# Graph attention over 412,500 edges: chunks of 1024 edges in place of 512

## Chip, cores, metric

One core of a Trainium2 chip runs the whole kernel. The time is the device time in microseconds from the start to the end of one execution. A version's time is the median of several runs.

## The reference

A graph has 12,500 nodes with 96 features, and 412,500 edges sorted by their destination. Each edge has 96 features of its own. There are 8 heads of 12 features.

```
Q, K, V = x @ Wq + bq, x @ Wk + bk, x @ Wv + bv        # per node
E       = edge_attr @ We + be                          # per edge
score   = exp(clip(sum_head(K[src] * Q[dst] / sqrt(12) * E), -5, 5))
wV      = segment_sum(V[src] * score, dst);  Z = segment_sum(score, dst)
out     = layernorm(x + wV / (Z + 1e-6))
```

## The kernel before

**Stages.** First the node tables are made: TensorE turns x and projects it; keys and values go to a table in DRAM (`kv_table`), queries as three bf16 parts to another (`q_table`). Beside it the destinations are loaded, turned and made relative to each chunk's least destination. Then comes the main loop over 806 chunks of 512 edges (`CHUNK`, 128 partitions by `G` = 4 edges), and last the output stage over 25 batches of 500 nodes: division, residual and layer norm.

**One chunk in the main loop.** The edges of a chunk have destinations in a window of `WIN` = 32 nodes, since they are sorted.
- SyncE loads edge features (`ea`) and destinations (`dst_b`) for half a ring, 4 chunks, at a time, and per chunk the query rows of the window (`q_win`, 106 rows). It may load when TensorE's step count says that the slots are free (L394).
- GpSimd gathers keys and values of the sources: one indirect DMA of 128 rows for each of the 4 edges of a partition (L530). It may do so when the message product of the chunk 8 before is done (L521). The indices are loaded by ScalarE's queue, 4 chunks at a time.
- ScalarE copies the turned edge features out of PSUM (`eaT`, L760), makes the matrix that selects each edge's query from the window (`away`, L765, then `ohT`, L768), and takes the exp of the scores (L757).
- TensorE turns the edge features (L631), projects them with We (L633), multiplies the selection by the window's queries (L640), and sums messages by destination with a 0/1 matrix (L647).
- VectorE multiplies keys by queries (L907) and by the projection (L915), adds within heads (L926), clips (L938), makes the 0/1 matrix `oh` (L910) and the messages (L919), and adds a chunk's sums to the accumulator (L934).

**Order.** Each engine's program is written out by hand in `step(s, u, ...)`, and `run_steps` puts 8 (ScalarE and GpSimd: 16) steps in a loop's body. In its step s TensorE turns chunk s, projects and selects for chunk s - 2 (`PROJ_LAG`), and sums chunk s - 5 (`SUM_LAG`); turning and projecting alternate matmul by matmul. The buffers between the engines are double. One signal is sent at the end of the step, and VectorE, ScalarE and SyncE all wait for that one:

```
                last.then_inc(pe_step, 1)                       # L650, TensorE
                dve.wait_ge(pe_step, a + PROJ_LAG + 1)          # L903, VectorE
                act.wait_ge(pe_step, s + 1)                     # L753, ScalarE
                at_least(pe, kqe_done, c - 1)                   # L628, TensorE waits for VectorE
```

VectorE makes the message of chunk s - 1 in the step in which it scores chunk s. ScalarE's step is exp of chunk s - 3, copy, measure and select of chunk s. A f32 matmul is two instructions with a weight load each (L633, L647), a transpose (L631) or a bf16 matmul (L640) one with one.

## Time and profile before

| | us |
|---|---|
| median of 3 runs | 5353.9 (5344.9 to 5357.64) |
| profiled execution | 5341.94 |
| its span, first to last instruction | 5340.3 |
| TensorE busy | 3563.3 (67%) |
| GpSimd busy | 3143.5 (59%) |
| VectorE busy | 2090.0 (39%) |
| ScalarE busy | 1722.8 (32%) |

The busy times are shares of one execution's span and overlap each other. A line name as L530 is a line of the kernel. PE is TensorE, PEld its weight loads, DVE VectorE, ACT ScalarE, POOL GpSimd, SP SyncE; a q behind the name means that the engine's sequencer acts, as when it issues a DMA.

### The profile page before, as it was taken

Reading aid. Unit: us, or ns where it says so; the run is one execution under the profiler, and the core shown is the slowest. Engines: PE = TensorE matmul, PEld = TensorE weight load, DVE = VectorE, ACT = ScalarE, POOL = GpSimd, SP = SyncE. Lnnn points to the kernel's source line nnn. Section 1 sums busy time; section 2 is a strip of 40 time slices with the busy share of each in tenths; the row PEclk is TensorE's granted clock in tenths of the full one; section 3 lists DMA queues with packets and bytes.
Section 4 is the critical chain, followed back from the end, with each engine's and each line's share of the span. In section 5 each row is a group of like instructions: output and inputs, shape, how many; then the busy total and the mean of one; then the engine's idle time right before and its main releaser. Section 6 shows DMA issues by size and latency. Waiting matters only on the chain.

```text
span 5340.3 us, 72730 instructions
## 1 busy us (share of the span) xinstructions
PE 3563.3 (67%) x19972; PEld 3422.0 (64%) x19973; DVE 2090.0 (39%) x5996; ACT 1722.8 (32%) x3602; POOL 3143.5 (59%) x3249
## 2 busy tenths in 40 slices
PE   7666666666666666666666666666666666666664
PEld 6666666666666666666666666666666666666663
DVE  4333334333333333333333433333334333433346
ACT  4332333323332332333233332333333232323337
POOL 4556656665666656656665666566566665666560
PEclk7555555555555555555555555555555555555555
DMA  7444444444444444444444444444444444444442
GB/s 227 107 109 110 119 109 109 111 118 109 109 111 117 110 108 111 116 111 109 111 116 112 109 112 113 113 109 111 110 118 109 110 115 113 109 110 116 112 109 84
DMA packets 497768, 607.49 MB, mean 114 GB/s; under 512 B 256053, under 2 KB 420224, under 8 KB 497630
## 3 DMA queue, kind: packets, MB, share of 16 engines
q0 software_dynamic: 155200, 318.39, 22.5%
q1 hardware_dynamic: 233215, 281.36, 18.0%
q10 hardware_dynamic: 109330, 7.48, 1.5%
q8 instruction: 9, 0.15, 0.0%
q14 instruction: 14, 0.11, 0.0%
HBM read 584.51 MB, written 22.46 MB: 114 GB/s over the span
## 4 chain that ended last, share of the span: by engine, by line
PE 51%; issue 27%; another core or an unknown queue 13%; DVE 4%; ACT 2%; DVEq 1%; DMA 0%; ACTq 0%; POOL 0%; SPq 0%; POOLq 0%
PE bank L633 18%; PE bank L647 17%; PE bank L631 11%; PE bank L640 5%; DVE kqe L915 2%; DVE raw_score L926 1%; DVEq L303 1%; ACT spare L814 0%; DVE oh L910 0%; ACT spare L802 0%; ACT accP L792 0%; PE bank L597 0%; ACT eaT L760 0%; DVE kqe L907 0%
## 5 line engine op out<-in xcount | busy, mean ns | idle before, releaser
L530 POOL DMA_INDIRECT kv<-kv_table,src_idx x3224 | 3118.9, 967 | 2059.6 <-DVE msg L919 1020.4
L633 PE MATMUL bank<-w_e,eaT 97*128 97x96 f32 x6448 | 1886.1, 391 | 282.1 <-issue 282.1
L631 PE MATMUL bank<-ident,ea 128*96 128x128 f32 x3224 | 1354.9, 421 | 920.4 <-issue 610.5
L633 PEld LDWEIGHTS bank<-w_e,eaT 97*128 97x128 f32 x6448 | 1778.6, 333 | 290.4 <-issue 288.8
L907 DVE TENSOR_TENSOR kqe<-kv,bank 128x384 f32<-128x384 f32 x806 | 446.4, 554 | 3157.5 <-remote 2428.7
L631 PEld LDWEIGHTS bank<-ident,ea 128*96 128x96 f32 x3224 | 806.2, 250 | 928.7 <-issue 594.5
L647 PE MATMUL bank<-oh,msg 128*104 128x32 f32 x6448 | 1276.8, 355 | 172.3 <-issue 170.0
L647 PEld LDWEIGHTS bank<-oh,msg 128*104 128x104 f32 x6448 | 1225.4, 290 | 168.7 <-issue 166.0
L757 ACT ACTIVATE msg<-score 128x32 f32<-128x32 f32 x806 | 184.8, 229 | 3504.8 <-remote 2565.3
L640 PEld LDWEIGHTS bank<-q_win,ohT 96*128 96x128 bf16 x3224 | 398.3, 154 | 414.5 <-issue 408.2
L640 PE MATMUL bank<-q_win,ohT 96*128 96x96 bf16 x3224 | 448.5, 279 | 299.6 <-issue 295.5
L765 ACT ACTIVATE away<-dst_b,minus_id 96x512 bf16<-96x512 int16 x806 | 581.1, 721 | 0.0
L768 ACT ACTIVATE ohT<-away 96x512 bf16<-96x512 bf16 x806 | 507.9, 630 | 25.5
L760 ACT COPY eaT<-bank 96x512 f32<-96x512 f32 x806 | 454.1, 563 | 4.6 <-PE bank L640 3.9
L919 DVE TENSOR_TENSOR msg<-kv,msg 128x384 f32<-128x384 f32 x806 | 442.9, 549 | 0.2 <-ACT msg L757 0.2
L915 DVE TENSOR_TENSOR kqe<-kqe,bank 128x384 f32<-128x384 f32 x806 | 439.9, 546 | 0.0
L926 DVE TENSOR_REDUCE raw_score<-kqe 128x32 f32<-128x384 f32 x806 | 437.9, 543 | 0.0
L910 DVE TENSOR_TENSOR oh<-iota,rel 128x128 f32<-128x128 f32 x806 | 231.2, 287 | 0.0
L938 DVE TENSOR_SCALAR score<-raw_score 128x32 f32<-128x32 f32 x806 | 187.4, 233 | 0.1
L934 DVE TENSOR_TENSOR accT<-bank,accT 104x32 f32 x806 | 144.2, 179 | 2.8 <-PE bank L647 2.3
L697 PE MATMUL bank<-ident,accP 104*125 104x104 f32 x100 | 29.0, 446 | 58.9 <-ACT accP L792 58.9
L697 PEld LDWEIGHTS bank<-ident,accP 104*125 104x125 f32 x100 | 22.8, 320 | 64.9 <-ACT accP L792 51.2
(81 smaller groups left out, 525.8 us busy)
## 6 DMA issues: line engine op xcount, KB each, us to landing
ea<-in_edge_attr_dram SPq DMA_DIRECT2D x201, 768.0 KB
dst_b<-dst_by_chunk SPq DMA_DIRECT2D x201, 384.0 KB
kv<-kv_table,src_idx POOLq DMA_INDIRECT x3224
q_win<-q_table SPq DMA_DIRECT2D x806, 19.9 KB
kv_table<-kv_out SPq DMA_DIRECT2D x25, 336.0 KB
q_table<-q_out SPq DMA_DIRECT2D x25, 252.0 KB
spare<-in_x_dram SPq DMA_DIRECT2D x25, 168.0 KB
out_dram<-spare SPq DMA_DIRECT2D x25, 168.0 KB
```

The source lines that it names most:

```text
L530: pool.indirect_dma_start(kv[:, slot, g, :], None, kv_dram[:, :], bass.IndirectOffsetOnAxis(ap=src_idx[:, u, g:g + 1], axis=0)).then_inc(k ...
L631: last = nc.tensor.transpose(eaT_ps[u % 2][0:D, g * P:(g + 1) * P], ea[:, u, g, :], ident[:, :])
L633: nc.tensor.matmul(e_ps[v % 2][:, g * D:(g + 1) * D], eaT[:, v % 2, g * P:(g + 1) * P], w_e[:, :], start=True, stop=True)
L640: last = nc.tensor.matmul(q_ps[v % 2][:, g * D:(g + 1) * D], sel[:, g, :], q_win[0:SEL, v, :], start=(g == 0), stop=(g == G - 1), skip_gro ...
L647: last = nc.tensor.matmul(sum_ps[w % 2][0:DZ, 0:WIN], msg[:, w % 2, g, :], oh[:, w % 2, g, :], start=(g == 0), stop=(g == G - 1))
L760: nc.scalar.copy(eaT[0:D, u % 2, :], eaT_ps[u % 2][0:D, :]).then_inc(eaT_copied, 1)
L765: nc.scalar.activation(away[:, :], dst_b[:, u % RING, :], ACT.Abs, bias=minus_id[:, bass.ds(s, 1)]).then_inc(away_done, 1)
L768: nc.scalar.activation(ohT[:, u % 2, :], away[:, :], ACT.Relu, bias=1.0, scale=-1.0).then_inc(ohT_built, 1)
L907: nc.vector.tensor_tensor(kqe[:, :, :], kv[:, ua, :, 0:D], q_ps[ua % 2][:, 0:G * D].rearrange("p (g d) -> p g d", g=G), ALU.mult).then_inc ...
L915: nc.vector.tensor_tensor(kqe[:, :, :], kqe[:, :, :], e_ps[ua % 2][:, 0:G * D].rearrange("p (g d) -> p g d", g=G), ALU.mult).then_inc(kqe_ ...
L919: nc.vector.tensor_tensor(msg[:, um % 2, :, 0:D].rearrange("p g (h d) -> p g h d", d=HD), kv[:, um, :, D:2 * D].rearrange("p g (h d) -> p ...
L926: nc.vector.tensor_reduce(raw_score[:, :], kqe[:, :, :].rearrange("p g (h d) -> p (g h) d", d=HD), AX_X, ALU.add).then_inc(heads_summed, 1)
```

## The change

A chunk is 1024 edges (`G` = 8), so there are 403, and its window 42 nodes; the window's query rows are 127. The ring has 4 chunks, half a ring 2, so the loads of edge features and the gathers ahead cover as many edges as before. A tile of 1024 f32 columns fills two banks of PSUM, so turning, queries and projection have one buffer each, and only the sums have two. TensorE's step is one chunk: turn it, sum the chunk 2 before, select its queries, project it; a signal follows the turning and another the projection. ScalarE copies when the first has come, and measures and selects for the next chunk, with the exp of the last one between them. VectorE waits for the second and makes scores and message of the same chunk in one step. The number of a chunk's further windows is found with a multiplication and a shift. `x_in` and `kv_out` of the first stage lie in the memory of `msg` and `kv`.

```diff
-G = 4
+G = 8
+GB = 4
-WIN = 32
-WIN_SHIFT = 5
+WIN = 42
+PER_WIN, PER_WIN_SHIFT = 1561, 16
-PROJ_LAG = 2
-SUM_LAG = 5
+SUM_LAG = 2
-SEL_READ = 106
-RING = 8
+SEL_READ = 127
+RING = 4
+ROUND = 8
...
-        eaT_ps, e_ps, q_ps, sum_ps = bank[0:2], bank[2:4], bank[4:6], bank[6:8]
+        eaT_ps, e_ps, q_ps = [ctx.enter_context(nc.psum_tensor(name, [P, 1024], F32)) for name in ("eaT_ps", "e_ps", "q_ps")]
+        sum_ps = [ctx.enter_context(nc.psum_tensor(f"sum_ps{i}", [P, 512], F32)) for i in range(2)]
...
-                sp.wait_ge(pe_step, s - HALF + PROJ_LAG)
+                sp.wait_ge(pe_projected, s - HALF)
...
+                if whole:
+                    if u % HALF == 0:
+                        ...
                     for g in range(G):
+                        last = nc.tensor.transpose(eaT_ps[0:D, g * P:(g + 1) * P], ea[:, u, g, :], ident[:, :])
+                    last.then_inc(pe_turned, 1)
                 if summing:
                     pe.wait_ge(msg_ready, n + 1)
-                    pe.wait_ge(oh_built, n + 1)
                     at_least(pe, acc_added, n - 1)
                     for g in range(G):
+                        last = nc.tensor.matmul(sum_ps[w][0:DZ, 0:WIN], msg[:, w, g, :], oh[:, w, g, :],
                                                 start=(g == 0), stop=(g == G - 1))
-                last.then_inc(pe_step, 1)
+                if whole:
+                    pe.wait_ge(ohT_built, s + 1)
+                    at_least(pe, kqe_done, s)
+                    landed(pe, q_win_in, s, u, 16)
+                    sel = ohT[:, u % 2, :].rearrange("n (p g) -> n g p", g=G)
+                    for g in range(G):
+                        nc.tensor.matmul(edge_rows(q_ps, g), sel[:, g, :], q_win[0:SEL, u, :],
+                                         start=(g % GB == 0), stop=(g % GB == GB - 1), skip_group_check=True)
+                    pe.wait_ge(eaT_copied, s + 1)
+                    for g in range(G):
+                        last = nc.tensor.matmul(edge_rows(e_ps, g), eaT[:, g * P:(g + 1) * P], w_e[:, :],
+                                                start=True, stop=True)
+                last.then_inc(pe_projected, 1)
...
+            def measure(s, u):
+                if u % HALF == 0:
+                    landed_half(act, s, u)
+                at_least(act, ohT_built, s)
+                nc.scalar.activation(away[:, :], dst_b[:, u, :], ACT.Abs, bias=minus_id[:, bass.ds(s, 1)]).then_inc(away_done, 1)
+
+            def select(s, u):
+                act.wait_ge(away_done, s + 1)
+                nc.scalar.activation(ohT[:, u % 2, :], away[:, :], ACT.Relu, bias=1.0, scale=-1.0).then_inc(ohT_built, 1)
+
             def step(s, u, _):
+                c, v = s - 1, (u - 1) % 2
+                coming = not isinstance(s, int) or s + 1 < C
+                if not isinstance(s, int) or s < C:
+                    act.wait_ge(pe_turned, s + 1)
+                    nc.scalar.copy(eaT[0:D, :], eaT_ps[0:D, :]).then_inc(eaT_copied, 1)
+                if coming:
+                    measure(s + 1, (u + 1) % RING)
                 if not isinstance(s, int) or 0 <= c < C:
                     act.wait_ge(score_ready, c + 1)
+                    nc.scalar.activation(msg[:, v, :, D:DZ],
+                                         score[:, v, :].rearrange("p (g h) -> p g h", g=G), ACT.Exp).then_inc(exp_done, 1)
+                if coming:
+                    select(s + 1, (u + 1) % RING)
...
+                dve.wait_ge(pe_projected, s + 1)
+                if scoring:
+                    landed(dve, kv_in, s, u, 16 * G)
+                    nc.vector.tensor_tensor(in_banks(kqe[:, :, :]), in_banks(kv[:, u, :, 0:D]), by_edge(q_ps), ALU.mult).then_inc(kq_done, 1)
+                    nc.vector.tensor_tensor(oh[:, h, :, :], ..., ALU.is_equal)
+                    dve.wait_ge(kq_done, s + 1)
+                    nc.vector.tensor_tensor(in_banks(kqe[:, :, :]), in_banks(kqe[:, :, :]), by_edge(e_ps), ALU.mult).then_inc(kqe_done, 1)
+                if not isinstance(s, int) or 0 <= n < C:
...
+                    nc.vector.tensor_tensor(acc, sum_ps[h][0:DZ, 0:WIN], acc, ALU.add).then_inc(acc_added, 1)
+                if scoring:
+                    dve.wait_ge(kqe_done, s + 1)
+                    nc.vector.tensor_reduce(raw_score[:, :], ..., AX_X, ALU.add).then_inc(heads_summed, 1)
+                    dve.wait_ge(heads_summed, s + 1)
+                    nc.vector.tensor_scalar(score[:, h, :], raw_score[:, :], -5.0, 5.0, ALU.max, ALU.min).then_inc(score_ready, 1)
+                    dve.wait_ge(exp_done, s + 1)
+                    nc.vector.tensor_tensor(msg[:, h, :, 0:D]..., kv[:, u, :, D:2 * D]..., msg[:, h, :, D:DZ]..., ALU.mult).then_inc(msg_ready, 1)
```

## Rows read from the trace of the kernel before

**Rows 1.** The page: busy us and share of the span; granted clock, 40 slices
```profile
PE 3563.3 (67%) x19972; PEld 3422.0 (64%) x19973; DVE 2090.0 (39%) x5996; ACT 1722.8 (32%) x3602; POOL 3143.5 (59%) x3249
...
PEclk7555555555555555555555555555555555555555
```

**Rows 2.** Groups by line, whole execution: line, engine, shapes, count | busy us, mean ns | idle
```profile
L530 POOL DMA_INDIRECT kv<-kv_table,src_idx x3224 | 3118.9, 967 | 2059.6 <-DVE msg L919 1020.4 <-issue 1006.7 <-DMA kv_table<-kv_out 32.4
L633 PE MATMUL bank<-w_e,eaT 97*128 97x96 f32 x6448 | 1886.1, 391 | 282.1 <-issue 282.1
...
L631 PE MATMUL bank<-ident,ea 128*96 128x128 f32 x3224 | 1354.9, 421 | 920.4 <-issue 610.5 <-DVE kqe L915 195.4 <-ACT eaT L760 107.9
L647 PE MATMUL bank<-oh,msg 128*104 128x32 f32 x6448 | 1276.8, 355 | 172.3 <-issue 170.0 <-DVE accT L934 1.0
```

**Rows 3.** Timeline of GpSimd: start us, us, line, [idle before <- what ended it]
```profile
2480.87 0.95 POOL L530 DMA_INDIRECT kv<-kv_table,src_idx  x1 [4.79 <-DVE msg L919]
...
2494.91 1.33 POOL L530 DMA_INDIRECT kv<-kv_table,src_idx  x1 [0.30 <-issue]
...
2500.30 0.95 POOL L530 DMA_INDIRECT kv<-kv_table,src_idx  x1 [0.30 <-issue]
2506.27 0.95 POOL L530 DMA_INDIRECT kv<-kv_table,src_idx  x1 [5.02 <-DVE msg L919]
```

**Rows 4.** Timeline of ScalarE in the same stretch, exp only
```profile
2484.01 0.23 ACT L757 ACTIVATE msg<-score 128x32 f32<-128x32 f32 x1 [1.19 <-PE bank L647]
...
2493.73 0.23 ACT L757 ACTIVATE msg<-score 128x32 f32<-128x32 f32 x1 [7.73 <-remote]
...
2503.78 0.23 ACT L757 ACTIVATE msg<-score 128x32 f32<-128x32 f32 x1 [8.06 <-remote]
```

**Rows 5.** Timeline of TensorE in the same stretch
```profile
2486.47 1.56 PE L647 MATMUL bank<-oh,msg 128*104 128x32 f32 x8
2487.84 0.43 PE L631 MATMUL bank<-ident,ea 128*96 128x128 f32 x1
2488.06 0.58 PE L633 MATMUL bank<-w_e,eaT 97*128 97x96 f32 x2
...
2490.52 1.56 PE L647 MATMUL bank<-oh,msg 128*104 128x32 f32 x8
2495.10 0.42 PE L631 MATMUL bank<-ident,ea 128*96 128x128 f32 x1 [3.02 <-ACT eaT L760]
...
2499.35 0.37 PE L631 MATMUL bank<-ident,ea 128*96 128x128 f32 x1 [2.28 <-issue]
```

**Rows 6.** Timeline at the end of the gathers, all engines
```profile
5216.27 0.95 POOL L530 DMA_INDIRECT kv<-kv_table,src_idx  x1 [0.30 <-issue]
...
5219.31 0.23 ACT L757 ACTIVATE msg<-score 128x32 f32<-128x32 f32 x1 [3.87 <-remote]
...
5223.81 1.56 PE L647 MATMUL bank<-oh,msg 128*104 128x32 f32 x8
...
5225.41 0.23 ACT L757 ACTIVATE msg<-score 128x32 f32<-128x32 f32 x1 [1.66 <-PE bank L647]
```

**Rows 7.** Groups by line, VectorE and ScalarE, whole execution
```profile
L765 ACT ACTIVATE away<-dst_b,minus_id 96x512 bf16<-96x512 int16 x806 | 581.1, 721 | 0.0
...
L760 ACT COPY eaT<-bank 96x512 f32<-96x512 f32 x806 | 454.1, 563 | 4.6 <-PE bank L640 3.9 <-PE bank L631 0.7
...
L907 DVE TENSOR_TENSOR kqe<-kv,bank 128x384 f32<-128x384 f32 x806 | 446.4, 554 | 3157.5 <-remote 2428.7 <-PE bank L647 577.0 <-issue 147.6
...
L910 DVE TENSOR_TENSOR oh<-iota,rel 128x128 f32<-128x128 f32 x806 | 231.2, 287 | 0.0
L938 DVE TENSOR_SCALAR score<-raw_score 128x32 f32<-128x32 f32 x806 | 187.4, 233 | 0.1
```

**Rows 8.** The page: DMA queues, packets, MB, share of 16 engines
```profile
q0 software_dynamic: 155200, 318.39, 22.5%
q1 hardware_dynamic: 233215, 281.36, 18.0%
```

More of the change, by code:

```diff
@@ L31 @@
 NP16 = 112
+NQ16 = 96
 BATCH = 4
@@ L39, in at_least, with run_steps @@
         engine.wait_ge(sem, value)
-def run_steps(engine, step, chunks, lag, round_values=None, from_round=0, unroll=RING, ahead=0):
+def run_steps(engine, step, chunks, lag, round_values=None, from_round=0, unroll=ROUND, ahead=0):
     rounds = (chunks - 1 - ahead) // unroll
@@ L299, in gnn_kernel, with load_bases @@
         IN_TAB = "these tables hold a chunk's least destination and how many further windows it has"
[L301 removed]
+        def load_bases(engine, first, count):
             return nc.values_load_multi_w_load_instructions(
[L304 removed]
+                base_tab[0:1, bass.ds(first, count)], engines=(engine.engine,), min_val=0, max_val=N - 1,
                 skip_runtime_bounds_check_because=IN_TAB)[1]
@@ L314, in further_pass @@
         def further_pass(engine, chunk, every=None):
-            reach = engine.value_load(most[0:1, 0:1], min_val=0, max_val=N // WIN)
+            reach = engine.value_load(most[0:1, 0:1], min_val=0, max_val=N // WIN + 1)
             with engine.If(reach > 0):
@@ L335, in within @@
         def within(node):
-            return nc.s_assert_within(node, 0, N - 1, skip_runtime_bounds_check_because=
-                                      "a chunk's windows end with the one that holds its greatest destination")
+            return nc.s_assert_within(node, 0, N_PAD - WIN, skip_runtime_bounds_check_because=
+                                      "a chunk's windows end with the one that holds its greatest destination or the next")
         def load_sources(engine, s, u):
@@ L581, in turn_destinations @@
                 pe.wait_ge(dst_float, 1)
-                for j in range(NJ):
-                    at_least(pe, rel_made, j - 1)
+                for t in range(TURNS):
+                    j, first = t * GB // G, t * GB % G
+                    at_least(pe, rel_made, t - 1)
                     rows = dst_nat[:, j * CHUNK:(j + 1) * CHUNK].rearrange("q (p g) -> q g p", g=G)
-                    for g in range(G):
-                        last = nc.tensor.transpose(bank[6 + j % 2][:, g * NQ:(g + 1) * NQ], rows[:, g, :], ident[0:NQ, 0:NQ])
+                    for g in range(GB):
+                        last = nc.tensor.transpose(bank[6 + t % 2][:, g * NQ:(g + 1) * NQ], rows[:, first + g, :], ident[0:NQ, 0:NQ])
                     last.then_inc(dst_turned, 1)
@@ L626, in step @@
-                if projecting:
-                    pe.wait_ge(eaT_copied, c + 1)
-                    at_least(pe, kqe_done, c - 1)
-                for g in range(G):
-                    if turning:
-                        last = nc.tensor.transpose(eaT_ps[u % 2][0:D, g * P:(g + 1) * P], ea[:, u, g, :], ident[:, :])
-                    if projecting:
-                        nc.tensor.matmul(e_ps[v % 2][:, g * D:(g + 1) * D], eaT[:, v % 2, g * P:(g + 1) * P],
-                                         w_e[:, :], start=True, stop=True)
@@ L660, in add_queries @@
                     for g in range(G):
-                        last = nc.tensor.matmul(q_ps[0][:, g * D:(g + 1) * D], sel[:, g, :], q_win[0:SEL, 0, :],
-                                                start=first and g == 0, stop=(g == G - 1), skip_group_check=True)
+                        last = nc.tensor.matmul(edge_rows(q_ps, g), sel[:, g, :], q_win[0:SEL, 0, :],
+                                                start=first and g % GB == 0, stop=(g % GB == GB - 1), skip_group_check=True)
                     last.then_inc(f_q_added, 1)
@@ L770, in step @@
+                if coming:
+                    select(s + 1, (u + 1) % RING)
                 if u % IDX_GROUP == 0:
                     load_sources(act, s + IDX_AHEAD, (u + IDX_AHEAD) % IDX_RING)
-            run_steps(act, step, C, 3, unroll=IDX_RING, ahead=IDX_AHEAD)
+            measure(0, 0)
+            select(0, 0)
+            run_steps(act, step, C, 1, unroll=IDX_RING, ahead=IDX_AHEAD)
             def further(c, extra):
                 taken(act, f_turned)
-                nc.scalar.copy(eaT[0:D, 0, :], eaT_ps[0][0:D, :]).then_inc(f_eaT_copied, 1)
+                nc.scalar.copy(eaT[0:D, :], eaT_ps[0:D, :]).then_inc(f_eaT_copied, 1)
```

214 lines of the change are left out of this document (93 added, 121 removed).

## The prediction, made before the changed kernel ran

> **What bounds the kernel now.** I read the busy times and the clock first [rows 1]. No engine is full: TensorE 67% at a granted clock of 0.5 (1.2 GHz), GpSimd 59%, VectorE 39%, ScalarE 32%. Then the groups by line [rows 2]. GpSimd issues 3224 gathers. Its 3118.9 us busy, 1006.7 us of short issue gaps and 1020.4 us of waiting for VectorE's message product (L919) add up to 5146.0 us, and that is all of the main loop. So the time is the gathers (4125.6 us, which no part of this change touches) plus 1020.4 us of waits, plus some 195 us ahead of the loop and behind it (5341.9 - 5146.0 = 195.9). Per 2048 edges (201.5 such rounds) that is 20.5 us of gathers and 5.06 us of waits.
>
> The timelines show where the wait comes from. GpSimd streams 16 gathers with 0.3 us gaps, stops 5.02 us, streams again [rows 3]. ScalarE's exp (L757) waits for TensorE's step signal and for scores made long before. Its starts say when the signal was seen: at once at 2484.01 (3.1 us after the stream began), but then only at 2493.73 and 2503.78 [rows 4]. The steps that these answer ended at 2488.03 and 2492.08 by TensorE's rows (start plus duration of L647) [rows 5]: the signals are 5.7 and 11.7 us late. TensorE itself runs full steps of 4.05 us meanwhile, idles 3.02 us for VectorE's answer, then trickles (issue gaps of 2.28 us) [rows 5]. The stream's last gather ended at 2501.25 and the held signal came 2.5 us later. After the last gather of all (end 5217.22) one signal comes 2.1 us later, and from there on each is seen 0.04 us after its step's end (5223.81 + 1.56 = 5225.37, exp at 5225.41) with all the other engines at full rate [rows 6]. So my reading: while gathers stream for more than 3.1 us, TensorE's signals queue behind its own instructions. Two late signals are 9.7 and 10.05 us apart and 48 TensorE instructions lie between them (24 matmuls and 24 weight loads a chunk: 8 + 4 + 8 + 4 by the counts of [rows 2] and L640, and 19972 in all [rows 1]): 0.2 us for each. About 2.2 us after a stream's end the queue is empty.
>
> The Trainium skill (Perfetto Trace Analysis, section Tensor Engine Instruction) says that the profile estimates a matmul's end and leaves the signal's way to the other engines out. By that rule the lateness could be arithmetic that the rows end too early; TensorE's own work would then be the bound, nothing of it changes, and the time stays. It is a rival below; the 0.04 us in the last rows speaks against it.
>
> **The change, part by part.** Per 1024 edges the gathers stay 8, the TensorE instructions stay 96. A sum matmul has 42 moving columns for 32: its interval of 0.17 us (1.37 us for 8 [rows 5]) goes with 104-column weight loads, so I take 0; at the other end 42/32 of it would be 0.05 x 16 = 0.9 us a chunk, which is in TensorE's slack of (12.6 - 8.1) us.
>
> TensorE's step is now turn, sum, queries, project. Turn: 8 x 0.22 = 1.75 us (2487.84 to 2488.06 [rows 5]); sum 2 x 1.37 = 2.74; the rest of 2 x 4.05, 3.6 us, is queries and projection. It still needs 8.1 us.
>
> VectorE per 1024 edges, from 0.287 us for 128 elements and 0.55 for 384 [rows 7], 1.03 ns an element: products, reduction and message of 768 elements 0.95 us each, the 336-element selection 0.50. Six fixed parts fall away, in an engine that is idle 61%: nothing. What counts is the chain from a signal to the next gather. Before: 2.5 us (2503.78 to 2506.27 [rows 3, 4]), since the message of the chunk before was ready to be made. After: product 0.95, selection 0.45, product 0.95, reduction 0.95, score 0.25, exp 0.3, message 0.95, then 0.8 to the gather's start, in all 5.65 us. Bounds: 5.0 with overlaps, 6.3 without.
>
> ScalarE's order is copy, measure, exp, select. The exp of a chunk stands behind the copy (0.56 us for 512 columns [rows 7]; 1.0, between 0.56 and 1.13) and the measure (0.72; 1.3, between 0.72 and 1.44) of the next chunk, which need the new turned signal. If that is late, the chain is 1.0 + 1.3 + 0.3 + 0.95 + 0.8 = 4.35 us from there.
>
> Single buffers: queries of chunk s wait for kqe of s-1, 2.4 us after the signal; turn and sum (4.5 us) lie beside it. With prompt signals this costs nothing; with a late one TensorE stops as it does now (3.02 us [rows 5]). Behind that waiting instruction stand only its own projection and the next turn.
>
> Now one round. Zero is the restart of gathers, the stream lasts 20.1, and 4 slots let two chunks go before the third needs a message. Let x be when the first projection ends. The next ends 8.1 later, and its signal is seen at S = 3.1 + 0.2 x (96 - 11.9 x (3.1 - x)) (11.9 instructions a us is 48 in 4.05). The turned signal has 16 instructions more: S + 3.2. Gathers restart at S + 3.2 + 4.35 = S + 7.6. For x of -0.4, 0.8 and 1.5, the values that follow each other when I go through the schedule, S is 13.9, 16.9, 18.5 and the restart 21.5, 24.5, 26.1: waits of 1.4, 4.4, 6.0, mean 3.9. SP's loads (4 for 6 a round, which crawl through the same stretch) I price at 0.8 more. So 4.7 us of wait for 5.06: 201.5 x 4.7 = 947 us for 1020, that is -73.
>
> The tail has two chunks of lag at 8.1 us where it had five steps at 4.05, and 5.65 for 2.5: +8. In the setup the destination tables are 4096 for 3584 columns, off the gathers' path (these begin at 71 us): 0, at most +5. A round's SP loads are larger (126 partitions of destinations for 96) and fewer; SP waits most of the time: 0.
>
> Sum: 5341.9 - 73 + 8 = 5277 us. The median of the runs shown lies 12.0 above the profiled execution: 5289; I say 5285.
>
> **Rivals.**
> 1. Slower: the message chain always starts from the emptied queue. Then each round waits 2.2 + 5.65 = 7.85 us, 2.8 more than now: +562 + 8, 5920 us. It decides once S passes about 20, and 96 instructions at 0.2 us are 19.2 already. It can also come in every second or third round (5500 to 5700). For it: the chain doubles, and two signals must pass where one did. Against: 5.65 us may overlap the drain.
> 2. Much faster: what fills the queue is the number of waits, signals and small instructions of all engines, which halve. Gathers never stop: 5341.9 - 1020 = 4322; half of it 4830. For it: SP crawls together with TensorE. Against: TensorE's 96 instructions are most of what is issued and stay.
> 3. No change: TensorE's rows end too early, or the hold depends on gathers alone: about 5354.
> 4. The query load of 127 partitions, for 106: by the Trainium skill (DMA: Bandwidth & Descriptors, section Why a DMA increments its semaphore by 16 and not by 1) such a load goes through one DMA engine, as no divisor above 1 is left. As a mechanism of this kernel: one engine moves 127 packets more a chunk; at the queue's mean of 0.18 x 16 x 5340 / 233215 = 0.066 us [rows 8] 8.4 us of a 12.6 us period, beside its share of the gathers' 22.5%. That could raise a period to 13.9 us, +1.2 x 403: 5830 us. The packets are 192 bytes and shorter than the mean, so little chance.
>
> **How the numbers follow.** My forecast's own range is 5000 to 5480 (wait 3.3 to 5.7 us), chance 0.46; rival 1 0.28, rival 2 0.13, rival 3 0.08, rival 4 0.05. A tenth left out at each end gives 4850 to 5650. A measurement of this kernel tells 0.2% (11 us) from no change. Faster: 0.34 of my case, 0.13, and 0.03 of rival 3: 0.50. Same: 0.06. Slower: 0.44.
>
> **What would show it.** The gather row keeps 3224 at 967 ns, and its wait for the message goes from 1020 to near 950 us. Streams of two chunks (20 us) with stops of 1.4 to 6 us; stops near 7.9 are rival 1, none is rival 2. TensorE's signals again prompt early in a stream and up to 10 us or more late in it. Messages 0.95 us, exp directly behind the measure where a stream ends. I am wrong if signals are no longer held though TensorE's instructions are the same, if a stop begins after one chunk of gathers (10 us), or if gathers wait for something other than the message.

## The result: 7.0% slower

The changed kernel takes 5725.3 us (median of 4 runs, 5700.7 to 5762.0) and the kernel before beside it 5353.2 us (4 runs): ratio 1.0701, 95% interval 1.0670 to 1.0732. The forecast was 5285 us in a range of 4850 to 5650, so the sign was wrong and the time lay outside the range. What came is rival 1, at a lower price than the 5920 us worked out for it.

The page of the profile after (busy us, share of the span; granted clock in 40 slices; DMA queues), beside [rows 1, 8]:

```profile
span 5698.9 us, 58267 instructions
...
PE 3357.8 (59%) x19976; PEld 3207.3 (56%) x19977; DVE 1916.4 (34%) x3179; ACT 1432.8 (25%) x1990; POOL 3126.2 (55%) x3249
...
PEclk7555555555566555555556555555555555555555
...
q0 software_dynamic: 155168, 318.18, 20.5%
q1 hardware_dynamic: 151850, 299.57, 16.3%
```

Every engine is busy for less time than before. The granted clock of TensorE is not lower either: the digits are cut down to tenths, and the mean over the span is 0.573 for 0.508, so a part of the time was at 2.4 GHz and the rest at 1.2 GHz. Only waiting grew. The groups by line of the kernel after (line, engine, shapes, count | busy us, mean ns | idle us before them and what ended it), beside [rows 2, 7]:

```profile
L550 POOL DMA_INDIRECT kv<-kv_table,src_idx x3224 | 3100.2, 962 | 2432.0 <-DVE msg L960 1448.3 <-issue 947.5 <-DMA kv_table<-kv 36.3
L665 PE MATMUL e_ps<-w_e,eaT 97*128 97x96 f32 x6448 | 1387.0, 397 | 390.8 <-issue 288.0 <-ACT eaT L789 101.3
...
L653 PE MATMUL sum_ps<-oh,msg 128*104 128x42 f32 x6448 | 1051.5, 323 | 580.9 <-issue 571.8 <-DVE msg L960 3.4
...
L777 ACT ACTIVATE away<-dst_b,minus_id 126x1024 bf16<-126x1024 int16 x403 | 462.5, 1148 | 0.0
L789 ACT COPY eaT<-eaT_ps 96x1024 f32<-96x1024 f32 x403 | 406.0, 1007 | 4030.5 <-remote 3017.3 <-PE eaT_ps L646 810.5 <-issue 202.6
...
L942 DVE TENSOR_TENSOR kqe<-kv,q_ps 128x768 f32<-128x768 f32 x403 | 384.5, 954 | 3240.8 <-remote 2658.6 <-issue 293.3 <-PE e_ps L665 288.8
```

GpSimd's wait for the message went from 1020.4 to 1448.3 us (+427.9); its gathers took 18.7 us less and its short issue gaps 59.2 less. The sum, +350.0, is all but 8.6 us of the 358.6 us by which the span grew (5340.3 to 5698.9). A round of 2048 edges now waits 7.19 us (1448.3 / 201.5) for 5.06, where I had said 4.7.

One cycle of the kernel after shows how, beside [rows 3 to 5]. The timeline (start us, us, engine, line, [idle before <- what ended it]), from the restart of the gathers to the next restart; first TensorE alone:

```profile
2960.73 1.49 PE L665 MATMUL e_ps<-w_e,eaT 97*128 97x96 f32 x6
...
2965.66 1.99 PE L665 MATMUL e_ps<-w_e,eaT 97*128 97x96 f32 x16
2967.49 1.20 PE L646 MATMUL eaT_ps<-ident,ea 128*96 128x128 f32 x7
...
2973.14 0.74 PE L653 MATMUL sum_ps<-oh,msg 128*104 128x42 f32 x3 [0.48 <-issue]
...
2979.48 0.23 PE L653 MATMUL sum_ps<-oh,msg 128*104 128x42 f32 x1 [1.02 <-issue]
```

and the other engines in the same stretch:

```profile
2961.09 0.94 POOL L550 DMA_INDIRECT kv<-kv_table,src_idx  x1 [8.48 <-DVE msg L960]
2962.35 0.95 DVE L942 TENSOR_TENSOR kqe<-kv,q_ps 128x768 f32<-128x768 f32 x1 [2.08 <-issue]
...
2979.89 0.95 POOL L550 DMA_INDIRECT kv<-kv_table,src_idx  x1 [0.30 <-issue]
2983.77 0.95 DVE L942 TENSOR_TENSOR kqe<-kv,q_ps 128x768 f32<-128x768 f32 x1 [16.61 <-remote]
2983.86 1.01 ACT L789 COPY eaT<-eaT_ps 96x1024 f32<-96x1024 f32 x1 [16.74 <-remote]
...
2984.64 0.50 DVE L943 TENSOR_TENSOR oh<-iota,rel 128x336 f32<-128x336 f32 x1
...
2985.06 0.95 DVE L946 TENSOR_TENSOR kqe<-kqe,e_ps 128x768 f32<-128x768 f32 x1
...
2986.04 0.95 DVE L955 TENSOR_REDUCE raw_score<-kqe 128x64 f32<-128x768 f32 x1
2987.02 0.19 DVE L958 TENSOR_SCALAR score<-raw_score 128x64 f32<-128x64 f32 x1
2987.25 0.26 ACT L794 ACTIVATE msg<-score 128x64 f32<-128x64 f32 x1 [1.34 <-DVE score L958]
...
2987.54 0.96 DVE L960 TENSOR_TENSOR msg<-kv,msg 128x768 f32<-128x768 f32 x1 [0.32 <-ACT msg L794]
2989.31 0.94 POOL L550 DMA_INDIRECT kv<-kv_table,src_idx  x1 [8.48 <-DVE msg L960]
```

The gathers restart at 2961.09. The projection of the chunk ends at 2967.65 (2965.66 + 1.99), 6.6 us into the stream, and VectorE starts on its signal only at 2983.77, 16.1 us late and 2.93 us after the stream's last gather ended (2980.84). It is the signal that is late and not VectorE: the trace has the time at which the semaphore was raised, 2983.74. Meanwhile TensorE works off the sum's matmuls one to three at a time with issue gaps between, and is through with them at 2979.71, 4 us before the signal. Then the chain runs its full length, product, selection, product, reduction, score, exp, message, while GpSimd stands still: 5.54 us to the restart. 2.93 + 5.54 is the 8.47 us of the stop.

The same cut for each kernel, by me, from the starts and ends of all gathers and of VectorE's first instruction behind a signal. It takes the stops of over 3 us without the first and the last, medians in us; "ratio" is the time over that of the kernel before on the same chip; "wait" is the gathers' wait for the message in the groups by line. The lines below the first two are explained with their experiments:

```
kernel                         stops  end to signal  signal to restart  wait    ratio to before
before                          204      2.19             2.50          1020.4      1
after                           174      2.83             5.55          1448.3      1.0701
e9  before, message first       244      2.22             1.57           984.1      0.9837
e10 after at 512 edges          247      2.27             3.73          1518.9      1.0783
e6  after, exp first            197      1.46             5.54          1481.5      1.0594
e8  after, bf16 projection      129      3.73             5.57          1193.7      1.0214
e12 e10, message a step later   369      1.79             1.37          1299.8      0.9979
e13 after, message a step later 169      2.99             1.77           933.0      0.9727
```

The streams before these stops differ much in length, 9.7 us in e12, 14.8 in e10, 20.4 before, 19.7 after and 30.3 in e8 (medians), and yet the signal comes 1.5 to 3.7 us after their end. So what ends the hold at a stop is mostly the end of the stream, and not a count of TensorE's instructions. It isn't a rule without exception: [rows 3, 4] have a late signal in the middle of a stream.

At the end of the gathers, beside [rows 6], the last signals of the kernel after:

```profile
5569.73 0.95 POOL L550 DMA_INDIRECT kv<-kv_table,src_idx  x1 [0.30 <-issue]
5571.45 0.95 DVE L942 TENSOR_TENSOR kqe<-kv,q_ps 128x768 f32<-128x768 f32 x1 [14.44 <-remote]
...
5574.72 3.73 PE L665 MATMUL e_ps<-w_e,eaT 97*128 97x96 f32 x16
5578.48 0.95 DVE L942 TENSOR_TENSOR kqe<-kv,q_ps 128x768 f32<-128x768 f32 x1 [1.64 <-PE e_ps L665]
```

The first of them answers a projection that ended at 5560.59 by TensorE's rows, 10.9 us earlier; the second comes 0.03 us after its projection's end (5574.72 + 3.73), with no gathers running.

### The profile page after: what moved, and what is told of

It is laid out like the page before. It is cut to its first block, busy times and chain, and to the rows that moved or that the text cites. A ratio compares the mean times of both kernels' runs of the same rounds, so it can differ in the third digit from the quotient of the medians.

```text
span 5698.9 us, 58267 instructions
## 1 busy us (share of the span) xinstructions
PE 3357.8 (59%) x19976; PEld 3207.3 (56%) x19977; DVE 1916.4 (34%) x3179; ACT 1432.8 (25%) x1990; POOL 3126.2 (55%) x3249
## 4 chain that ended last, share of the span: by engine, by line
PE 44%; issue 33%; another core or an unknown queue 16%; ACT 5%; DVE 1%; DMA 0%; ACTq 0%; SPq 0%; POOL 0%; DVEq 0%; POOLq 0%
PE e_ps L665 19%; PE sum_ps L653 13%; PE eaT_ps L646 9%; PE q_ps L661 4%; ACT away L777 1%; ACT ohT L781 1%; ACT eaT L789 1%; ACT spare L833 0%; ACT spare L845 0%; ACT accP L823 0%; ACT msg L794 0%; DMA spare<-in_dst_dram 0%; DVE q_rest L921 0%; PE e_ps L595 0%
## 5 line engine op out<-in xcount | busy, mean ns | idle before, releaser
L550 POOL DMA_INDIRECT kv<-kv_table,src_idx x3224 | 3100.2, 962 | 2432.0 <-DVE msg L960 1448.3
L665 PE MATMUL e_ps<-w_e,eaT 97*128 97x96 f32 x6448 | 1387.0, 397 | 390.8 <-issue 288.0
L665 PEld LDWEIGHTS e_ps<-w_e,eaT 97*128 97x128 f32 x6448 | 1306.7, 305 | 408.1 <-issue 296.2
L942 DVE TENSOR_TENSOR kqe<-kv,q_ps 128x768 f32<-128x768 f32 x403 | 384.5, 954 | 3240.8 <-remote 2658.6
L789 ACT COPY eaT<-eaT_ps 96x1024 f32<-96x1024 f32 x403 | 406.0, 1007 | 4030.5 <-remote 3017.3
L653 PE MATMUL sum_ps<-oh,msg 128*104 128x42 f32 x6448 | 1051.5, 323 | 580.9 <-issue 571.8
L653 PEld LDWEIGHTS sum_ps<-oh,msg 128*104 128x104 f32 x6448 | 1040.6, 247 | 598.6 <-issue 587.3
L646 PE MATMUL eaT_ps<-ident,ea 128*96 128x128 f32 x3224 | 729.8, 394 | 95.7 <-issue 90.6
L646 PEld LDWEIGHTS eaT_ps<-ident,ea 128*96 128x96 f32 x3224 | 598.7, 194 | 147.9 <-issue 123.7
L960 DVE TENSOR_TENSOR msg<-kv,msg 128x768 f32<-128x768 f32 x403 | 386.2, 958 | 426.4 <-ACT msg L794 284.6
L777 ACT ACTIVATE away<-dst_b,minus_id 126x1024 bf16<-126x1024 int16 x403 | 462.5, 1148 | 0.0
L781 ACT ACTIVATE ohT<-away 126x1024 bf16<-126x1024 bf16 x403 | 420.4, 1043 | 0.1
L958 DVE TENSOR_SCALAR score<-raw_score 128x64 f32<-128x64 f32 x403 | 90.0, 223 | 13.9
L715 PE MATMUL eaT_ps<-ident,accP 104*125 104x104 f32 x100 | 29.0, 446 | 59.2 <-ACT accP L823 59.2
```

The source lines that it names most:

```text
L550: pool.indirect_dma_start(kv[:, slot, g, :], None, kv_dram[:, :], bass.IndirectOffsetOnAxis(ap=src_idx[:, u, g:g + 1], axis=0)).then_inc(k ...
L646: last = nc.tensor.transpose(eaT_ps[0:D, g * P:(g + 1) * P], ea[:, u, g, :], ident[:, :])
L653: last = nc.tensor.matmul(sum_ps[w][0:DZ, 0:WIN], msg[:, w, g, :], oh[:, w, g, :], start=(g == 0), stop=(g == G - 1))
L665: last = nc.tensor.matmul(edge_rows(e_ps, g), eaT[:, g * P:(g + 1) * P], w_e[:, :], start=True, stop=True)
L777: nc.scalar.activation(away[:, :], dst_b[:, u, :], ACT.Abs, bias=minus_id[:, bass.ds(s, 1)]).then_inc(away_done, 1)
L781: nc.scalar.activation(ohT[:, u % 2, :], away[:, :], ACT.Relu, bias=1.0, scale=-1.0).then_inc(ohT_built, 1)
```

## The experiments

Times are medians; each kernel ran on one chip with the kernel before beside it. Not all chips are alike: on one, the kernel before takes 4277 us instead of 5350, and e1 to e5 ran there. Across chips the ratios are compared, and a difference of 1 to 2% between two ratios from two chips is not shown by that: the kernel before itself takes 5349 us on the chip of e6, e8, e10 and e11 and 5440 on that of e12 to e15.

**e1, one gather of eight.** The changed kernel; the other seven eighths of the keys and values are a constant.

```diff
-                for g in range(G):
+                for g in range(1):
                     pool.indirect_dma_start(kv[:, slot, g, :], None, kv_dram[:, :],
```

> The changed kernel, but GpSimd issues only the first of a chunk's 8 gathers; the other seven eighths of the keys and values are a constant, filled in once. Theory (TensorE's signals are held while gathers stream): with 1.25 us of gather per chunk there is no stream, both signals of a chunk are seen within 0.1 us, and the loop goes at TensorE's own pace: 8.1 us a chunk at 1.2 GHz, down to about 5.5 us where the clock is 2.4 GHz, so 2500 to 3500 us in all. Rival (the single buffers or the order of the step bind): signals are prompt or not, but the time stays above 4500 us. Rival (signals late for another reason, as the query load of 127 rows on one DMA engine): signals stay 10 us late with one gather a chunk.

2546.8 us, beside 4277 for the kernel before. On this chip that said only that the gathers bound the kernel, since here no signal was late with all gathers either (e5). It is one run. It is repeated as e11.

**e2, query loads of 128 rows instead of 127** (`SEL_READ = 128`) in the changed kernel.

> The changed kernel with 128 query rows loaded per chunk for 127. Theory (held signals and the longer chain): 5725 within 1%, the stops of the gathers stay near 7 to 8.4 us. Rival 4 of the prediction (127 rows go through one DMA engine, 128 through sixteen): below 5500.

4346.8 us, ratio 1.0170 (1.0145 to 1.0194), against 1.0148 for the unchanged e5 on this chip. Rival 4 is out: the load of 127 partitions costs nothing that can be measured here.

**e3, the kernel before with windows of 42 nodes** (`WIN = 42`, `SEL_READ = 127`).

> The kernel before with windows of 42 nodes for 32 (selection over 126 partitions, 127 query rows, 42 sum columns), chunks still 512. Theory: nothing in the chain from TensorE's signal to the next gather changes: 5353 within 1%, gather wait near 1020 us. Rival (the wider window costs, by its loads or by the sums' columns): 5450 or more.

4290.0 us, ratio 1.0038 (1.0023 to 1.0054). Wider windows cost 0.4% where gathers never stop.

**e4, the new schedule at chunks of 512 edges.** The changed kernel with the chunks of before; the windows stay at 42 nodes.

```diff
-G = 8
-GB = 4
+G = 4
+GB = 2
-RING = 4
+RING = 8
```

> The changed kernel's order of work, single buffers and two signals, but with chunks of 512 edges and a ring of 8. Theory (after the end of a stream the stop is 2.2 us of emptying plus the chain signal to message to gather): the chain is 0.55 + 0.25 + 0.55 + 0.55 + 0.23 + 0.25 + 0.55 + 0.8 = 3.7 us, so stops near 5.9 us, every 4 to 5 chunks: 5350 to 5500 us. Rival (single buffers alone cost the 372 us): 5650 or more. Rival (the size of the chunk alone costs it, the order gains): below 5300.

4265.5 us, ratio 0.9975 (0.9965 to 0.9986). The expectation was for a chip where gathers stop, and is tested by e10.

**e5, the changed kernel again**, on the chip of e1 to e4.

> The changed kernel itself, beside the kernel before on the same chip. The four runs above stood beside a kernel before of 4277 us where it had taken 5353, and there the gathers never stopped. Theory (the loss of the change is the stop after a stream whose signals are held): where the kernel before takes about 5350, the ratio is 1.07 and the gathers stop 7 us; where it takes about 4280, nothing is held and the changed kernel is bound by the gathers too: 4280 to 4350, ratio 1.00 to 1.02. Rival (the longer chain or the single buffers cost by themselves): ratio 1.05 or more beside a kernel before of 4280 as well.

4340.4 us, ratio 1.0148 (1.0130 to 1.0166). Its groups by line:

```profile
L550 POOL DMA_INDIRECT kv<-kv_table,src_idx x3224 | 3154.2, 978 | 1037.6 <-issue 979.7 <-DMA kv_table<-kv 36.4 <-DVE msg L960 21.4
L942 DVE TENSOR_TENSOR kqe<-kv,q_ps 128x768 f32<-128x768 f32 x403 | 384.6, 954 | 2187.4 <-DMA kv<-kv_table,src_idx 2006.2 <-PE e_ps L665 169.2 <-issue 11.9
```

Here GpSimd waits 21.4 us for messages in the whole run, and VectorE waits for gathers, never for a late signal ("remote", 2658.6 us above). The change costs 65 us all the same: the gathers take 978 ns for e4's 956, 22 x 3224 = 71 us. So on this chip the longer gathers come with the larger chunk (e4 to e5), not with the schedule. Why a gather is longer beside chunks of 1024 wasn't isolated.

**e9, the kernel before with the message first.** VectorE makes selection matrix and message ahead of the product of keys and queries.

```diff
                 dve.wait_ge(pe_step, a + PROJ_LAG + 1)
+                if messages:
+                    (selection matrix, then the message)
                 if scores:
                     landed(dve, kv_in, a, ua, 16 * G)
...
                                             e_ps[ua % 2][:, 0:G * D].rearrange("p (g d) -> p g d", g=G), ALU.mult).then_inc(kqe_done, 1)
-                if messages:
-                    (the message)
```

> The kernel before, its chunks of 512 edges, windows and signals unchanged; alone the order of VectorE's instructions in a step is another: the projected half of the values and the message (with the selection matrix) are made ahead of the product of keys, queries and edge keys, where before they come behind it. Theory (the message chain that starts from the emptied TensorE queue sets the gathers' restart): where gathers stand still between streams, each stop of about 4.7 us gets shorter by the VectorE work that no longer lies between the signal and the gathers' release, 0.5 to 0.8 us; over some 200 stops 100 to 160 us less. Where gathers never stop (the time before is near 4280 us instead of 5350), the message's place sets nothing: within 0.3% of before. Rival (keys and values come in last, the message's release is never what the gathers wait for): no change under either condition. Rival (the scores, now made later, hold ScalarE's exp and through it the next message): slower by 0.5 us a step, some 200 us.

5266.2 us beside 5341.9, ratio 0.9837 (0.9791 to 0.9882). From signal to restart it is 1.57 us for 2.50, 0.9 less and not 0.5 to 0.8, but there were 244 stops for 204, so the gain was 76 us and not 100 or more. What stands between signal and gather is paid for; a shorter stop buys shorter streams.

**e10, e4 again where gathers stop.**

> The changed kernel's schedule alone (transposes ahead of the sum, single buffers of turned features, queries and projection, the two TensorE signals of a chunk) at chunks of 512 edges, a ring of 8 and windows of 32 nodes: the kernel of the fourth run again, wanted where the kernel before takes about 5350 us and its gathers stand still between streams. Theory (a round now costs the hold of TensorE's signals and one chain signal, message, gather; the chain's ends are per chunk, so that at half a chunk each VectorE step is about half as long): chain 6.2 us at 1024 edges becomes about 4 us, and the loss against before is between none and a third of the changed kernel's 372 us: 5350 to 5500. Rival (the size of the chunk costs nothing, the order and the single buffers do it): 5700. Where gathers never stop: 0.9975 of before, as measured.

(The windows were 42 nodes here too, not 32 as this text says.) 5766.5 us beside 5349.1, ratio 1.0783 (1.0757 to 1.0810). My expectation (5350 to 5500) fell and its rival stood: the loss comes with the schedule, whatever the chunk's size. The chain is shorter at 512 edges, 3.73 us for 5.55, and the stops are more, 247 for 174: 1518.9 us of waiting.

**e6, exp ahead of the measuring.** In the changed kernel.

```diff
-                if coming:
-                    measure(s + 1, (u + 1) % RING)
                 if not isinstance(s, int) or 0 <= c < C:
                     act.wait_ge(score_ready, c + 1)
                     (exp)
+                if coming:
+                    measure(s + 1, (u + 1) % RING)
```

> The changed kernel; alone ScalarE's order is another: the exponentials of a chunk come ahead of the measuring of distances for the next chunk (1148 ns each) instead of behind it. Theory (gathers wait on the chain signal, products, scores, exp, message): where gathers stop, each of some 190 stops loses up to the 1.1 us of the measuring if it lies between, 100 to 200 us less than the changed kernel's 5725. Rival (the measuring is done by the time the scores come, the exp waits for VectorE alone): no change against the changed kernel. Rival (the next selection matrix comes later, TensorE is later with the next chunk's queries): 1.1 us a chunk, up to 400 us more. Where gathers never stop: ratio to before 1.015, as the changed kernel there.

5658.9 us, ratio 1.0594 (1.0565 to 1.0623): 57 us better than the changed kernel by the ratios ((1.0701 - 1.0594) x 5349), half of what the theory asked. The chain is the same 5.54 us, so the measuring is not in it: both held signals come together (2983.77 above, ScalarE's copy at 2983.86; 0.09 us apart in the median of the changed kernel's stops) and the exp waits for VectorE's score (1.34 us in the row). The wait for the message is even longer, 1481.5 us for 1448.3, since only 1 of 200 streams is three chunks long, for 34 of 188. The gain is in GpSimd's issue gaps (947.5 to 882.7 us) and gathers (3100.2 to 3080.3). Half of what the gaps lose is one kind, some 1.9 us between a chunk's first gather and its second: 18 of them in the changed kernel, one here. Why they go is open.

**e8, the projection in bf16.** In the changed kernel, with less precise edge keys: 8 loads and 8 matmuls for 16 and 16.

```diff
-        eaT = sb("eaT", [DA, CHUNK])
+        eaT = sb("eaT", [DA, CHUNK], BF16)
+        w_e16 = sb("w_e16", [DA, D], BF16)
-                        last = nc.tensor.matmul(edge_rows(e_ps, g), eaT[:, g * P:(g + 1) * P], w_e[:, :],
+                        last = nc.tensor.matmul(edge_rows(e_ps, g), eaT[:, g * P:(g + 1) * P], w_e16[:, :],
```

> The changed kernel with the turned edge features and their weights in bf16, so that the projection is 8 loads and 8 products a chunk instead of 16 and 16 (80 TensorE instructions instead of 96); the precision of the edge keys is lower. Theory (the signals are held while TensorE's instructions queue behind the gathers' streams, a fixed time for each instruction): 16 of 96 fewer, each round's hold shorter by about a sixth, 1 us and more of the 7.2 us: 150 to 300 us below the changed kernel. Rival (the hold depends on the gathers' stream alone and not on TensorE's instructions): the same wait of 7.2 us a round, and no more than 50 us less from the shorter projection. Where gathers never stop: ratio to before 1.015.

5458.7 us beside 5349.1, ratio 1.0214 (1.0189 to 1.0238): 260 us less than the changed kernel by the ratios. The size is as the theory had it, the reason is not: no hold is shorter. The signal comes 3.73 us after the stream's end for 2.83, and from there to the restart it is 5.57 us for 5.55. But 123 of 135 streams are three chunks long, where 34 of 188 are in the changed kernel and most have two, so 129 stops remain of 174. My reading, not tested further: with fewer TensorE instructions, one more signal gets out before the hold.

**e11, e1 again where gathers stop.**

> The changed kernel with one of the eight gathers of a chunk; the other seven eighths of the keys and values are a constant. Wanted where the kernel before takes about 5350 us. Theory (TensorE's signals are held by the gathers' streams and by nothing else): with gathers at an eighth no signal is seen more than 1 us after the instruction's end, and the time falls to where TensorE bounds it, near the 2547 us measured on the other device. Rival (the signals are held by this device whatever the gathers do, for example at TensorE's load): signals still seen 5 us and more late, time 3500 and more.

2846.1 us beside 5349.1. Two groups and one step of its timeline:

```profile
L553 POOL DMA_INDIRECT kv<-kv_table,src_idx x403 | 383.6, 952 | 2260.2 <-DVE msg L963 2224.2 <-issue 35.1 <-POOL kv L539 0.9
...
L945 DVE TENSOR_TENSOR kqe<-kv,q_ps 128x768 f32<-128x768 f32 x403 | 384.5, 954 | 685.1 <-PE e_ps L668 604.7 <-issue 63.4
```

```profile
1505.69 3.70 PE L668 MATMUL e_ps<-w_e,eaT 97*128 97x96 f32 x16
1506.63 0.95 POOL L553 DMA_INDIRECT kv<-kv_table,src_idx  x1 [5.08 <-DVE msg L963]
1509.43 0.96 DVE L945 TENSOR_TENSOR kqe<-kv,q_ps 128x768 f32<-128x768 f32 x1 [3.61 <-PE e_ps L668]
```

The signal is seen 0.04 us after the projection's end (1505.69 + 3.70 to 1509.43); nine in ten of all are seen within 0.14 us, the rest within 1.43. With an eighth of the gathers nothing is held, on the chip on which e6, with all of them, has its signals 12 us late in the median of its stops: the hold goes with the stream of gathers. The time, one run again, is 300 us more than the 2547 expected; the granted clock was 0.726 here and 0.838 in e1.

**e12 and e13, the message a step later.** The one part of the new schedule that e10 left: VectorE again makes the message of the chunk before, from scores that are ready, and makes it first after the signal. e12 is e10 with it, e13 the changed kernel with it; single buffers, TensorE's order and the two signals stay.

```diff
                 dve.wait_ge(pe_projected, s + 1)
+                if not isinstance(s, int) or 1 <= s <= C:
+                    hm, um = (u - 1) % 2, (u - 1) % RING
+                    dve.wait_ge(exp_done, s)
+                    (message from kv[:, um] into msg[:, hm])
                 if scoring:
...
-                    dve.wait_ge(exp_done, s + 1)
-                    (message from kv[:, u] into msg[:, h])
```

> The schedule of the changed kernel at chunks of 512 edges and a ring of 8 (5766 us, where the kernel before takes 5349), and one thing undone: the message of a chunk is made a step later, as the first thing VectorE does when TensorE's signal of the next chunk is seen, as the kernel before makes it from scores that are already there. Single buffers, order on TensorE and the two signals stay. Theory (the loss is the length of the chain from the signal to the gathers' release): the stop between streams falls from 6.0 us to about the 3.8 us of the kernel before with the message first, and the time to 5250 to 5400, within 2% of before. Rival (the loss comes of the single buffers and the order on TensorE, which make its backlog longer or its signals later): 5600 to 5770, the stops stay near 6 us or become more. Where gathers never stop (before near 4280 us): 0.9975 of before, as without the edit.

> The changed kernel itself (1024 edges, windows of 42) with the same one thing undone: the message of a chunk is made a step later, first thing after the signal. Theory: stops fall from 8.4 us to the 2.2 us of TensorE's draining plus some 2.2 us of message and gather, 4.4 us; 5300 to 5450, most of the 372 us lost come back. Rival (single buffers and order): 5650 and more. A second effect on the same side as the rival: keys and values are held a step of 1024 edges longer out of 4096, so that gathers can run less far ahead: streams of one chunk rather than two, up to twice the stops, 5700. Where gathers never stop: 1.015 of before or, by the second effect, up to 1.05.

e12: 5425.8 us beside 5439.6, ratio 0.9979 (0.9962 to 0.9996). e13: 5285.6, ratio 0.9727 (0.9685 to 0.9770). From e10 to e12 the ratio falls by 0.080, from the changed kernel to e13 by 0.097: with this part undone, the change is 2.7% faster than before. The group and a stop of e13:

```profile
L550 POOL DMA_INDIRECT kv<-kv_table,src_idx x3224 | 3185.6, 988 | 1933.2 <-issue 963.0 <-DVE msg L943 933.0 <-DMA kv_table<-kv 37.2
```

```profile
2970.98 0.95 POOL L550 DMA_INDIRECT kv<-kv_table,src_idx  x1 [0.30 <-issue]
2975.00 0.96 DVE L943 TENSOR_TENSOR msg<-kv,msg 128x768 f32<-128x768 f32 x1 [11.81 <-PE e_ps L665]
2975.88 0.95 DVE L949 TENSOR_TENSOR kqe<-kv,q_ps 128x768 f32<-128x768 f32 x1
...
2976.77 0.94 POOL L550 DMA_INDIRECT kv<-kv_table,src_idx  x1 [4.85 <-DVE msg L943]
```

The signal still comes after the stream's end (3.07 us here, 2.99 in the median), and then only the message, 0.96 us, lies before the restart: 1.77 us for 5.54. But in about half of the stops (89), this one among them, no signal of the projection is held; the projection itself is late:

```profile
2957.97 1.92 PE L646 MATMUL eaT_ps<-ident,ea 128*96 128x128 f32 x8
2965.96 1.01 ACT L789 COPY eaT<-eaT_ps 96x1024 f32<-96x1024 f32 x1 [10.38 <-issue]
2967.02 2.45 PE L665 MATMUL e_ps<-w_e,eaT 97*128 97x96 f32 x10 [4.28 <-ACT eaT L789]
2974.44 0.52 PE L665 MATMUL e_ps<-w_e,eaT 97*128 97x96 f32 x1 [0.40 <-issue]
```

The turning ends at 2959.89 and ScalarE copies its result 6.1 us later; then the projection's 16 matmuls take 7.9 us, with issue gaps, for the 3.70 us that they take in e11. VectorE starts 0.04 us after their end (2974.96). The wait falls from 1448.3 to 933.0 us, while the gathers themselves take 85 us more (988 ns for 962). Two things were moved at once, the message by a step and to the front of it. They weren't run apart on this schedule; on the kernel before the second alone brings 1.6% (e9), so by subtraction most of the 8 to 10% is the first. Against e9 (0.9837), which has the message first too, e13 is lower by 1.1%, but on another chip. That slots are held a step longer shows as 41 streams of one chunk for 9, but it doesn't decide.

**e14 and e15, both kernels with the message first and the projection in bf16.** e14 is e9 with e8's edit, e15 is e13 with it.

> The kernel before with the message first (5266 us against 5342) and with the projection in bf16 (4 loads and 4 products fewer for 512 edges, 40 TensorE instructions instead of 48; lower precision of the edge keys). Theory (TensorE's backlog of instructions behind the streams sets when its signals are seen): as the bf16 projection brought 266 us on the changed kernel, 150 to 300 us here, 4970 to 5120. Rival (the shorter chain and the shorter backlog are covered by the same wait): within 50 us of 5266.

> The changed kernel with both: message a step later and first, projection in bf16. Theory (both terms add): 5459 minus what the message's place brings in the kernel without bf16; if that is 300 us, 5150. Rival (held keys and values shorten the streams): 5450 to 5700.

e14: 5280.0 us beside 5439.6, ratio 0.9708 (0.9672 to 0.9744), 1.3% below e9's from another chip, where 3 to 6% were expected. GpSimd waits no less for the message, 1035.6 us for e9's 984.1, so that the bf16 projection gains anything here is not shown. TensorE waits 1043.8 us for VectorE's products, which the message now stands ahead of (507.2 in e9, 195.4 in [rows 2]):

```profile
L633 PE MATMUL bank<-ident,ea 128*96 128x128 f32 x3224 | 1053.4, 418 | 1592.3 <-DVE kqe L926 1043.8 <-issue 538.5 <-DMA ea<-in_edge_attr_dram 8.1
```

e15: 5203.2 us, ratio 0.9570 (0.9534 to 0.9605), the lowest of all; it pays with the precision of the edge keys, and e13 has the lowest ratio of those that don't. The two gains don't add up: the bf16 projection is worth 4.9% on the changed kernel (e8) and 1.6% on e13, where a stop costs less. On this one chip e15 is 1.4% below e14, which differs from it by the rest of the change alone; so with the message made first, 1024 edges and their schedule do gain.

## Why the prediction was wrong

**What bounds the kernel: right.** Gathers plus their waits are the loop in both kernels, and 350.0 of 358.6 us of the loss are in that one row.

**The chain: right.** 5.65 us were predicted from signal to restart, with bounds of 5.0 and 6.3 (its terms add up to 5.60); the median is 5.55. VectorE's durations were within 0.05 us, the measure was 1.148 us for 1.3 and the copy 1.007 for 1.0. But the branch through copy and measure, which my formula used (S + 3.2 + 4.35), is not the one that ends a stop: both signals come together, and VectorE's chain is the longer (e6).

**The hold: right in kind.** The signals are held while gathers stream and are prompt without them (the end of the run above, e11). Rival 3 in its form by the Trainium skill (Perfetto Trace Analysis, section Tensor Engine Instruction: a matmul's end is estimated, and the signal's way is not in the record) can't account for 16.1 us in one place and 0.03 in another of the same trace; e9 and e13 show besides that what stands behind the signal moves the time.

**The failed step: "its signal is seen at S = 3.1 + 0.2 x (96 - 11.9 x (3.1 - x))".** I took the hold for a queue of TensorE's own instructions that empties at 0.2 us each while the gathers stream. That gave 13.9, 16.9 and 18.5 us into a stream of 20.1, so that much of the 5.65 us would lie beside gathers, and a mean wait of 3.9. Measured from the start of the stream, the signal that releases the gathers is seen at 22.6 us in the median, after the stream's end in 89% of the stops, and the wait is 2.83 + 5.55 us.

No count of instructions mends it, at whatever rate. In the cycle above the projection before ended 1.1 us into the stream (2960.73 + 1.49), where the formula gives 17.6; the signal was seen at 22.7. From 2968.88 to 2979.71 TensorE gets through one transpose and 16 sum matmuls with as many loads, 34 instructions in 10.8 us or 0.32 us each, and with that rate the formula gives 26.3. A rate between the two would hit 22.7, but TensorE was through with all that it had 4 us before the signal, and by the formula the next turned signal comes 3.2 us later, where it comes 0.09 us later in the median of the stops. What stands in its place is the stream's end, with the signals 1.5 to 3.7 us behind it in every kernel of the table. The 0.2 us came from intervals of 9.7 and 10.05 us in the kernel before, and the first of these begins with a signal that was prompt (2484.01), so only one of them is between two late signals.

Also, 8.1 us from one projection's end to the next was TensorE's pace at 1.2 GHz; in the cycle above it is 5.4 us (2962.22 to 2967.65), with a mean granted clock of 0.80 from 2961 to 2968. By the formula that would have made the signal earlier, and it wasn't.

I had written that rival 1 decides once S passes about 20 and that 96 instructions at 0.2 us "are 19.2 already", within 5% of the turning point, and still gave rival 1 0.28 against 0.46.

**Rival 1's price: too high by 195 us.** 5920 against 5725. In the profiled runs, of 1582 us of waits (201.5 x 7.85) 1448 came: 34 of 188 streams are three chunks long, which the one-round schedule had no room for. And gathers and issue gaps were 78 us less than the 4125.6 I had kept; in e6 another order on ScalarE alone took 65 us more from the gaps.

**Single buffers, signals, windows: priced at nothing, perhaps 1.4% together.** e12 has them all at chunks of 512 and stands at 0.9979, where e9, with the same message order and none of them, stands at 0.9837; but these are two chips, so the 1.4% is an estimate. e3 gives the wider windows 0.4% on the fast chip, the rest isn't divided. The larger chunk then brings 2.5% (e12 to e13, one chip), with 169 stops for 369. The gain that I forecast is there, but the message in the chunk's own step takes more than it gives. I had priced that move as a longer chain, correctly, and laid a part of it beside the stream, wrongly.

**Rival 4** is out by e2; the Trainium skill (DMA: Bandwidth & Descriptors, section Why a DMA increments its semaphore by 16 and not by 1) sends such a load through one DMA engine, and the traces agree: the load's semaphore is raised by the DMA about twice for each load of 127 rows in e5 and 16 times for each of 128 rows in e2, and the load lands 8.3 us after its issue for 6.3 (medians). Nothing waits for it long enough to be seen in the time.

**Open:** what in the gathers' stream holds TensorE's instructions and signals (e11 takes away gathers, their DMA traffic and GpSimd's work together), and why on one chip the same streams hold nothing. It isn't the loading of code: the changed kernel's trace has no packet of an instruction queue between 506 and 5577 us.

## What to carry to other kernels

When a software-pipelined loop loses a step of lag, ask what the shorter lag puts between the late event and the engine that bounds the loop: here 3 us more of VectorE and ScalarE work in each of 174 stops cost 7%, with every engine less busy than before. A delay read from two events is no rate: where the forecast turns on whether a held signal lands before or after the end of a stream, count many cycles first, measured from the stream's end as well as from its start. And after a change that loses, undo its parts one at a time before giving it up: with the message made a step later and first, this one was 2.7% faster than the kernel before.

## What the chip showed that was not expected

- The same program takes 4277 us on one chip and 5342 to 5440 us on three others. On the fast one the gathers' row waits 21.4 us for messages where it waits 1448.3 on another (the changed kernel), and no TensorE signal is late; one gather takes about the same (978 and 962 ns).
- So a change can have another sign on another chip: the new schedule at 512 edges is 0.9975 there and 1.0783 here.
- Streams of 10 us and of 30 us both have TensorE's held signals some 2 to 4 us after their end (1.79 us in e12, 3.73 in e8).
- Shorter stops are partly given back: in e9 each stop is 0.9 us shorter and there are 40 more of them.
